# Surplus row products of the last pair beside the scores in the run-out of the L2 heads

## The chip, the cores and the metric

The kernel runs on one core of a Trainium2 chip (trn2). The metric is the device time in microseconds, taken as the median of several runs. The engines are named as the profile names them: PE is TensorE (matmul) and PEld its weight loads, DVE is VectorE, ACT is ScalarE, POOL is GpSimd, SP is SyncE, which issues the DMAs.

## The reference

Four conditioned blocks L0 to L3 are computed one after the other on `x` of shape (2, 1024, 256) in float32. The change lies in the attention heads of block L2 (16 heads of width 16, batch 2, sequence 1024):

```python
qkv = (h @ Wqkv.T + bqkv).reshape(B, N, num_heads, hd, 3)
q, k, v = ...                                     # each (B, 16, 1024, 16)
energy = jnp.einsum('bhqd,bhkd->bhqk', q, k)
att = jax.nn.softmax(energy, axis=-1) / D ** 0.5
out = jnp.einsum('bhqk,bhkd->bhqd', att, v)
out = jnp.moveaxis(out, 1, 2).reshape(B, N, D)
out = out @ Wp.T + bp
```

The rest of L2 (a conditioned norm ahead of it, and a residual with a second norm behind it) and the other three blocks (L0 a cumulative-sum attention, L1 attention and MLP, L3 attention with 16 heads of width 64 and a mixture of experts) are not touched.

## The kernel before, in words

The program is a chain of stages with a barrier of all engines between them. Stage `l2h` computes the L2 heads, class `NarrowPairs`; `layer2_out` follows it, and begins when the last result of the heads has been stored to DRAM.

There are B*H = 32 heads, taken in N = 16 pairs. The two heads of a pair lie on two halves of the partitions: head h = 0 on partitions 0 to 47, h = 1 on 64 to 111 (line 1425, `r = 64 * h`), so that TensorE can multiply for both at once, each on its own half of the array's rows. The contraction has 48 rows (`SPLIT`): the high and low parts of q and k in three blocks of 16.

Per pair m and tile of 128 rows (TB = 8 tiles) there are three kinds of work on TensorE:

- `row(m, t, h, c)`, lines 1424 to 1433: the products of 128 queries with 512 keys, into the double bank `rowb[h]`. DVE reduces each full `rowb[h]` (128x1024) to a negated maximum per query (line 1483, `maxes`). With c == 0 the product waits until DVE has read the bank's former content.
- `score(m, k, h, c)`, lines 1435 to 1442: the transposed products (128 keys by 512 queries, 50 rows: two more hold the maxima as a shift), into one of three banks `score`. ACT takes the exponential of each into `pT` (line 1516). A score product waits for the exponential of the bank's former content (`exps`).
- `mix(m, k)`, lines 1444 to 1455: exponentials times values, into bank `out`, over the whole 128 rows, 8 matmul instructions for one k.

The order on TensorE is written out in `pe_program`, lines 1457 to 1469: for each turn m from -2 to 16 and each k from 0 to 7 it issues, phase 0: row and score alternately for c = 0, 1, then `mix` of the k two steps back (`LAG`), then phase 1: row and score again for c = 0, 1. In a phase the row product is of head `phase` and the score product of head `1 - phase`, so the two lie on different halves of the rows. This is called a step below; it has four row products, four score products and one mix. Row products run 12 steps ahead of the scores (`ahead`, line 1368: the pair after next in the second half of a turn). So in turn 14 from k = 4 on and in turn 15, 12 steps in all, there are no row products left: `there(mr)` is false. These 12 steps, with the two mixes and the copy of the result (line 1501, `ocopy`) in turn 16, are called the run-out. When the last maximum of a pair is there, DVE turns the 16 columns of maxima (lines 1490 to 1495), and SP places them by eight small DMAs into the two extra rows of Q (line 1406, `place_shift`); the first score of the pair waits for them (line 1439).

GpSimd copies values (`staged`), early; ACT does the exponentials and one `ocopy` per pair; SP loads the pairs ahead, stores the results and places the shifts.

Of the kernel before, what the change touches and what calls it, by code (L numbers as in the profile page):

```python
# [21 lines left out]
P = 128  # L22
B, S, D = 2, 1024, 256
T = B * S // P
TB = S // P
KF = D // P
C = 512
# [1303 lines left out]
class NarrowPairs:  # L1331
# [91 lines left out]
    def pe_program(self, pe):  # L1423
        def row(m, t, h, c):
            u, r = m % self.SLOTS, 64 * h
            if c == 0:
                if t == 0:
                    pe.wait_ge(self.loaded[u], (m // self.SLOTS + 1) * 16 * self.LOADS)
                self.need(pe, self.maxes, (TB * m + t) * 2 + h - 1)
            mm = pe.matmul(self.rowb[h][:, c * C:(c + 1) * C], self.Q[r:r + self.SPLIT, u, t * P:(t + 1) * P],  # L1430
                           self.K[r:r + self.SPLIT, u, c * C:(c + 1) * C], start=True, stop=True)
            if c == 1:
                mm.then_inc(self.rowsums, 1)

        def score(m, k, h, c):
            u, r = m % self.SLOTS, 64 * h
            v = 4 * (TB * m + k) + 2 * (1 - h) + c
            if k == 0 and h == 1 and c == 0:
                pe.wait_ge(self.shifted, 8 * 16 * (m + 1))
            self.need(pe, self.exps, v - 2)  # L1440
            pe.matmul(self.score[v % 3][:, :], self.K[r:r + self.SPLIT + 2, u, k * P:(k + 1) * P],  # L1441
                      self.Q[r:r + self.SPLIT + 2, u, c * C:(c + 1) * C], start=True, stop=True).then_inc(self.scores, 1)

        def mix(m, k):
            g = TB * m + k
            pe.wait_ge(self.exps, 4 * (g + 1))
            if k == 0:
                pe.wait_ge(self.staged, m + 1)
                self.need(pe, self.ocopied, m)
            for h in range(2):  # L1450
                for c in range(2):
                    r = self.mw * (2 * h + c)
                    mm = pe.matmul(self.ob[r:r + self.mw, :], self.vs[:, m % self.SLOTS, h, k, :],  # L1453
                                   self.pT[:, g % 4, h, c * C:(c + 1) * C], start=k == 0, stop=k == TB - 1)
            mm.then_inc(self.mixed, 1)

        for m in self.TURNS:
            for k in range(TB):
                mr, tr = self.ahead(m, k)
                for phase in range(2):  # L1460
                    for c in range(2):
                        if self.there(mr):
                            row(mr, tr, phase, c)
                        if self.there(m):
                            score(m, k, 1 - phase, c)
                    if phase == 0:
                        mine, kk = (m, k - self.LAG) if k >= self.LAG else (m - 1, k - self.LAG + TB)
                        if self.there(mine):
                            mix(mine, kk)
# [1098 lines left out]
```

## Time and profile before

| | us |
|---|---|
| median of 3 runs | 2332.14 (2328.83 to 2342.71) |
| the profiled execution's own time | 2340.13 |
| its span in the trace | 2338.4 |
| PE busy | 1969.7 (84% of the span) |
| DVE busy | 1423.3 (61%) |
| ACT busy | 1117.9 (48%) |
| mean granted clock of TensorE | 0.896 |

A busy share is an average over stages with different limits; only the rows of the stage around the change tell what it is worth. PE is counted busy while a matmul is in flight, whatever part of the array it uses. PEclk is the granted clock of TensorE as a share of its full 2.4 GHz: 1.00 is 2.4 GHz, 0.50 is 1.2 GHz, and these are its two levels; a number between them in a window is a mixture. Times in rows are counted from the start of the span. The stage of the L2 heads goes from about 695 us to 1090 us.

### The profile page before, as it was taken

To read this page: it belongs to the slowest core of one execution; us is meant where nothing else is said; L and a number is where in the kernel's file an instruction comes from. 1 tells how busy PE (TensorE), PEld (TensorE's weight loads), DVE (VectorE), ACT (ScalarE), POOL (GpSimd) and SP (SyncE) were. 2 spreads that over 40 slices of the span, in tenths; PEclk is the share of its full clock that TensorE was granted. 3 is DMA by queue.
4 is the path that set the end of the run, shared out by engine and by line. 5 is a ranking of instruction groups with operands and counts; after the bars stand their busy time and mean duration, and the time that the engine had idled before them with its cause. 6 is when DMAs were issued, how large, how long until landed. Compare 5 with 4: busy or idle time off the path is not lost. (4 is left out here: it accounts for less than half of the span.)

```text
span 2338.4 us, 34514 instructions
## 1 busy us (share of the span) xinstructions
PE 1969.7 (84%) x12926; PEld 1155.3 (49%) x12926; DVE 1423.3 (61%) x2514; ACT 1117.9 (48%) x2013; POOL 737.9 (32%) x703
## 2 busy tenths in 40 slices
PE   6988589679649999995499949999999999794776
PEld 2444367568323333331345525555555555483676
DVE  5432543453448999960756638777777777317665
ACT  1111133231214888873256538777777777303243
POOL 2221340064003000001235535444444444103476
PEclk8999799889776999995699969999999999895688
DMA  5000000100143211102036783445444444242153
GB/s 158 0 1 0 16 7 1 38 1 1 54 135 99 47 36 49 49 7 77 7 116 216 221 223 86 113 113 113 113 113 111 110 109 109 91 149 103 31 160 81
DMA packets 197254, 190.96 MB, mean 82 GB/s; under 512 B 65440, under 2 KB 155936, under 8 KB 196832
## 3 DMA queue, kind: packets, MB, share of 16 engines
q1 hardware_dynamic: 194016, 184.56, 29.4%
q0 software_dynamic: 3072, 4.20, 0.9%
q8 instruction: 103, 1.69, 0.3%
q14 instruction: 63, 0.52, 0.1%
HBM read 121.07 MB, written 67.37 MB: 81 GB/s over the span
## 5 line engine op out<-in xcount | busy, mean ns | idle before, releaser
L1293 DVE TENSOR_REDUCE l3h_nmax<-l3h_score 128x1 f32<-128x1024 f32 x256 | 313.5, 1225 | 152.7 <-PE l3h_score L1236 152.7
L1327 POOL TENSOR_SCALAR l3h_prob<-l3h_prob,l3h_inv 128x1024 f32<-128x1024 f32 x256 | 288.3, 1126 | 340.6 <-DVE l3h_inv L1299 340.6
L1516 ACT ACTIVATE l2h_pT<-l2h_score 128x512 f32<-128x512 f32 x512 | 266.3, 602 | 118.6 <-PE l2h_score L1441 116.7
L1483 DVE TENSOR_REDUCE l2h_nm<-l2h_rowb 128x1 f32<-128x1024 f32 x256 | 301.0, 1217 | 31.8 <-PE l2h_rowb L1430 31.8
L1317 ACT ACTIVATE l3h_prob<-l3h_score,l3h_nmax 128x1024 f32<-128x1024 f32 x256 | 286.1, 1117 | 48.2 <-DVE l3h_nmax L1293 13.2
L1259 PE MATMUL l3h_out<-l3h_pT,l3h_vs 128*64 128x512 f32 x1024 | 274.4, 617 | 0.0
L1236 PE MATMUL l3h_score<-l3h_K,l3h_Q 64*128 64x512 f32 x1536 | 249.1, 430 | 26.2 <-DMA l3h_K<-l_k 24.3
L1236 PEld LDWEIGHTS l3h_score<-l3h_K,l3h_Q 64*128 64x128 f32 x1536 | 125.8, 186 | 238.0 <-issue 190.1
L1430 PE MATMUL l2h_rowb<-l2h_K,l2h_Q 48*128 48x512 f32 x512 | 183.0, 470 | 40.8 <-DMA l2h_K<-l_k 29.8
L1441 PE MATMUL l2h_score<-l2h_Q,l2h_K 50*128 50x512 f32 x512 | 206.0, 491 | 3.5 <-ACT l2h_pT L1516 3.5
L1285 ACT ACTIVATE l3h_pT<-l3h_ring 128x512 f32<-128x512 f32 x256 | 152.8, 597 | 100.9 <-PE l3h_ring L1247 100.4
L1247 PEld LDWEIGHTS l3h_ring<-ident,l3h_prob 64*128 64x128 f32 x4096 | 172.1, 139 | 37.0 <-issue 8.0
L1897 PE MATMUL l3qkv_bank<-w3qkvT,l3qkv_norm_out 128*128 128x512 f32 x384 | 174.4, 598 | 0.9 <-ACT l3qkv_norm_out L690 0.9
L1430 PEld LDWEIGHTS l2h_rowb<-l2h_K,l2h_Q 48*128 48x128 f32 x512 | 81.4, 199 | 189.1 <-DVE l2h_nm L1483 140.8
L1283 DVE COPY l3h_pT<-l3h_ring 128x512 f32<-128x512 f32 x256 | 172.1, 672 | 2.0 <-PE l3h_ring L1247 2.0
L1247 PE MATMUL l3h_ring<-ident,l3h_prob 64*128 64x64 f32 x4096 | 169.3, 222 | 2.2 <-DVE l3h_pT L1283 1.8
L1453 PE MATMUL l2h_out<-l2h_pT,l2h_vs 128*32 128x512 f32 x1024 | 148.2, 654 | 0.0
L1981 POOL TENSOR_TENSOR l3qkv_lo<-l3qkv_full,l3qkv_hi 128x512 fp32r<-128x512 f32 x64 | 102.3, 1625 | 133.6 <-ACT l3qkv_hi L1917 133.6
L1441 PEld LDWEIGHTS l2h_score<-l2h_Q,l2h_K 50*128 50x128 f32 x512 | 85.8, 195 | 63.3 <-ACT l2h_pT L1516 46.5
L1897 PEld LDWEIGHTS l3qkv_bank<-w3qkvT,l3qkv_norm_out 128*128 128x128 f32 x384 | 70.2, 192 | 72.8 <-issue 71.1
L1528 POOL COPY l2h_vs<-V 128x128 f32<-128x128 f32 x32 | 8.3, 294 | 255.3 <-PE l2h_out L1453 255.3
L1958 DVE TENSOR_SCALAR l3qkv_full<-l3qkv_bank,headln 128x512 f32<-128x512 f32 x64 | 50.5, 808 | 58.6 <-PE l3qkv_bank L1883 40.1
(355 smaller groups left out, 3364.3 us busy)
## 6 DMA issues: line engine op xcount, KB each, us to landing
l3h_Q<-l_q SPq DMA_DIRECT2D x128, 256.0 KB, 4.6
l3h_K<-l_k SPq DMA_DIRECT2D x128, 128.0 KB, 4.9
l_v<-l3qkv_v SPq DMA_DIRECT2D x16, 512.0 KB, 4.1
l_q<-l3qkv_hi SPq DMA_DIRECT2D x32, 256.0 KB, 2.8
l_q<-l3qkv_lo SPq DMA_DIRECT2D x32, 256.0 KB, 2.9
l_k<-l3qkv_hi SPq DMA_DIRECT2D x32, 256.0 KB, 3.7
l_k<-l3qkv_lo SPq DMA_DIRECT2D x32, 256.0 KB, 3.7
l3h_vs<-l_v SPq DMA_DIRECT2D x32, 256.0 KB, 3.5
```

Source lines behind the costliest of these rows:

```text
L1236: mm = pe.matmul(self.score[t % 2][:, c * C:(c + 1) * C], self.Q[r, u, x, t * P:(t + 1) * P], self.K[r, u, y, :], start=i == 0, stop=i == 2)
L1247: mm = pe.transpose(self.ring[half][:, kk * P // 2:(kk + 1) * P // 2], self.prob[r, g % 4, kk * P:(kk + 1) * P], self.ident[r, r])
L1259: mm = pe.matmul(self.ob[n % 2][c * self.hd:(c + 1) * self.hd, :], self.vs[:, n % 2, kk, :], self.pT[:, n % 2, kk, c * C:(c + 1) * C], sta ...
L1283: eng.tensor_copy(dst, src).then_inc(self.emptied_d, 1)
L1293: dve.tensor_reduce(self.nmax[:, t % 4:t % 4 + 1], self.score[t % 2][:, :], AX.X, ALU.max, negate=True).then_inc(self.maxes, 1)
L1317: act.activation(self.prob[:, q, :], self.score[g % 2][:, :], ACT.Exp, bias=self.nmax[:, q:q + 1], accum_out=self.total[:, q:q + 1]).then_ ...
L1327: pool.tensor_scalar(self.prob[:, q, :], self.prob[:, q, :], self.inv[:, q:q + 1], self.vscale, ALU.mult, ALU.mult).then_inc(self.scaled, 1)
L1430: mm = pe.matmul(self.rowb[h][:, c * C:(c + 1) * C], self.Q[r:r + self.SPLIT, u, t * P:(t + 1) * P], self.K[r:r + self.SPLIT, u, c * C:(c ...
L1441: pe.matmul(self.score[v % 3][:, :], self.K[r:r + self.SPLIT + 2, u, k * P:(k + 1) * P], self.Q[r:r + self.SPLIT + 2, u, c * C:(c + 1) * C ...
L1483: dve.tensor_reduce(self.nm[:, mr % 2, at:at + 1], self.rowb[h][:, :], AX.X, ALU.max, negate=True).then_inc(self.maxes, 1)
L1516: act.activation(self.pT[:, g % 4, h, c * C:(c + 1) * C], self.score[v % 3][:, :], ACT.Exp).then_inc(self.exps, 1)
L1897: mm = pe.matmul(bank[2 + j][:, :], nt.out[:, c, kf, t * P:(t + 1) * P], wT[:, (kf * 6 + j) * C:(kf * 6 + j + 1) * C], start=kf == 0, stop ...
```

## The change

A new function `again` in `pe_program` issues one row product of the last pair (m = 15, in slot 3), with no semaphore increment, into `rowb[h]`. It is called where a row product would stand, for the steps in which none is left but scores are: the pair index `mr` is 16 or 17 and m is 14 or 15. These are 12 steps with four products each, 48 in all. Each is preceded by a wait until DVE has made all 256 maxima, which is after the last read of `rowb`. The operands are those of earlier row products of pair 15, and the results are not read.

```diff
@@ -1432,6 +1432,12 @@
             if c == 1:
                 mm.then_inc(self.rowsums, 1)
 
+        def again(t, h, c):
+            u, r = (self.N - 1) % self.SLOTS, 64 * h
+            pe.wait_ge(self.maxes, 2 * TB * self.N)
+            pe.matmul(self.rowb[h][:, c * C:(c + 1) * C], self.Q[r:r + self.SPLIT, u, t * P:(t + 1) * P],
+                      self.K[r:r + self.SPLIT, u, c * C:(c + 1) * C], start=True, stop=True)
+
         def score(m, k, h, c):
@@ -1461,6 +1467,8 @@
                     for c in range(2):
                         if self.there(mr):
                             row(mr, tr, phase, c)
+                        elif mr >= self.N and self.there(m):
+                            again(tr, phase, c)
                         if self.there(m):
                             score(m, k, 1 - phase, c)
```

## Rows read from the trace of the kernel before

**Rows 1.** Page, the span in 40 slices of 58.5 us

```profile
PE   6988589679649999995499949999999999794776
PEclk8999799889776999995699969999999999895688
```

**Rows 2.** Windows: us; busy PE, PEld, DVE, ACT, POOL; PEclk, DMA share, GB/s

```profile
744.00:1036.00 292.00, 285.89 (x1768) 100.53 (x1765) 265.18 (x260) 235.47 (x454) 6.38 (x24) 1.00 0.17 41
...
1036.00:1042.00 6.00, 4.89 (x29) 1.43 (x25) 1.94 (x5) 4.74 (x10) 0.00 (x0) 1.00 0.01 1
1042.00:1086.00 44.00, 41.55 (x135) 10.36 (x135) 0.00 (x0) 21.83 (x43) 0.00 (x0) 0.50 0.02 4
```

**Rows 3.** Waits between 1042 and 1086 us, the longest

```profile
ACT l2h_pT L1516 <- PE l2h_score L1441: 17.8, 9, 2.0
```

**Rows 4.** Timeline around the last row products: start us, us, engine, line

```profile
1033.57 2.07 ACT L1516 ACTIVATE l2h_pT<-l2h_score 128x512 f32<-128x512 f32 x4 [0.54 <-PE l2h_score L1441]
...
1034.64 1.07 PE L1453 MATMUL l2h_out<-l2h_pT,l2h_vs 128*32 128x512 f32 x8
...
1035.64 0.49 PE L1430 MATMUL l2h_rowb<-l2h_K,l2h_Q 48*128 48x512 f32 x1
...
1035.64 0.49 PE L1441 MATMUL l2h_score<-l2h_Q,l2h_K 50*128 50x512 f32 x1
...
1036.17 2.07 ACT L1516 ACTIVATE l2h_pT<-l2h_score 128x512 f32<-128x512 f32 x4 [0.54 <-PE l2h_score L1441]
1036.40 1.23 DVE L1483 TENSOR_REDUCE l2h_nm<-l2h_rowb 128x1 f32<-128x1024 f32 x1 [0.24 <-PE l2h_rowb L1430]
...
1036.83 0.50 PE L1441 MATMUL l2h_score<-l2h_Q,l2h_K 50*128 50x512 f32 x1 [0.24 <-ACT l2h_pT L1516]
...
1037.25 1.06 PE L1453 MATMUL l2h_out<-l2h_pT,l2h_vs 128*32 128x512 f32 x8
...
1038.25 0.73 PE L1441 MATMUL l2h_score<-l2h_Q,l2h_K 50*128 50x512 f32 x3
1038.31 5.21 SPq L1406 DMA_DIRECT2D l2h_Q<-l2h_shift  x8
...
1039.87 1.06 PE L1453 MATMUL l2h_out<-l2h_pT,l2h_vs 128*32 128x512 f32 x8
```

**Rows 5.** Timeline of the run-out at the low clock, and its end

```profile
1046.74 1.94 PE L1453 MATMUL l2h_out<-l2h_pT,l2h_vs 128*32 128x512 f32 x8
...
1048.61 1.22 PE L1441 MATMUL l2h_score<-l2h_Q,l2h_K 50*128 50x512 f32 x3
...
1079.27 1.94 PE L1453 MATMUL l2h_out<-l2h_pT,l2h_vs 128*32 128x512 f32 x8
...
1081.97 1.08 ACT L1516 ACTIVATE l2h_pT<-l2h_score 128x512 f32<-128x512 f32 x2 [1.99 <-PE l2h_score L1441]
...
1085.99 0.60 ACT L1501 ACTIVATE l2h_osb<-l2h_out 128x512 f32<-128x512 f32 x1 [2.94 <-PE l2h_out L1453]
```

**Rows 6.** Copies of the result at line 1501, one per pair, steady

```profile
1009.25 0.60 ACT L1501 ACTIVATE l2h_osb<-l2h_out 128x512 f32<-128x512 f32 x1
1030.48 0.60 ACT L1501 ACTIVATE l2h_osb<-l2h_out 128x512 f32<-128x512 f32 x1
```

**Rows 7.** Timeline of PE in the run-in of the stage

```profile
731.48 0.79 PE L1430 MATMUL l2h_rowb<-l2h_K,l2h_Q 48*128 48x512 f32 x1 [0.17 <-DVE l2h_nm L1483]
731.49 0.79 PE L1441 MATMUL l2h_score<-l2h_Q,l2h_K 50*128 50x512 f32 x1
...
732.64 1.93 PE L1453 MATMUL l2h_out<-l2h_pT,l2h_vs 128*32 128x512 f32 x8
...
736.71 1.86 PE L1453 MATMUL l2h_out<-l2h_pT,l2h_vs 128*32 128x512 f32 x8
738.50 0.50 PE L1430 MATMUL l2h_rowb<-l2h_K,l2h_Q 48*128 48x512 f32 x1
```

## The prediction

> **What bounds the kernel now.** I read the page's forty slices first [rows 1]. TensorE is the busiest engine, and its granted clock is full in most slices; the eighteenth and nineteenth slice, which reach from 994 to 1111 us, show PEclk fall to 9 and 5. The change lies at the end of the L2 heads, so I cut that stretch into windows [rows 2]. From 744 to 1036 us, while row products, scores and mixes all run, the clock is 1.00 (2.4 GHz) without a break. From 1036 to 1042 us it is still 1.00, with TensorE busy 4.89 of 6 us: there the last row products have just gone. From 1042 to 1086 us it is 0.50 (1.2 GHz), DVE does nothing, and ACT is busy 21.8 of 44 us. The list of waits names what ends last there: ACT waits 17.8 us in nine pieces of up to 2.0 us for a score product [rows 3]. In the run-out TensorE at the low clock sets the pace, and ACT, which has the same four exponentials per step as before, idles for half of it.
>
> The timeline gives the price of a step. Up to the last row products the mixes start at 1034.64 and 1037.25 us, a step of 2.61 us; the first step without row products is 1037.25 to 1039.87, 2.62 us, still at the full clock [rows 4]. So the row products cost nothing while they are there: a row and a score product begin together at 1035.64 and both take 0.49 us, on the two halves of the rows [rows 4]. What limits a step at the full clock is the loop of ACT and TensorE: four exponentials take 2.07 us and are followed by 0.54 us of waiting for the next score, 2.61 together [rows 4]. At the low clock the mixes at 1046.74 and 1079.27 us lie eight steps apart, 4.07 us each [rows 5]: a mix takes 1.94 us instead of 1.06 and three scores 1.22 instead of 0.73 [rows 4, 5].
>
> **The change part by part.** Nothing is removed and nothing moved; 48 products and 48 waits are added to TensorE's queue, none to another queue.
>
> First, the clock. After the change TensorE does in each of the 12 steps just what it did in the steady part: four products of 48 rows on one half, four scores on the other, a mix. In the steady part that held 1.00 for 292 us [rows 2], and in the run-in, row and score pairs with a mix between them at 732.64 us stood ahead of the rise, which the trace shows at 738.50, where a row product takes 0.50 instead of 0.79 us [rows 7]. Without the row products the clock fell about six us after the last of them. I take it that 1.00 holds to the last step. The mix of turn 15, k = 7 comes 11 steps after the one at 1037.25. At 2.61 us these are 28.7 us, and 0.1 more for the one copy of a result among them, so it would start at 1066.05 instead of 1079.27: 13.2 us less. The steady pitch of whole pairs, 1030.48 less 1009.25 = 21.23 us for eight steps, is 2.65 per step [rows 6] and would give 12.8; it holds row waits on DVE that the run-out has not, so I take 13.2 and keep 12.8 as an end.
>
> Second, the end. From that last stepped mix to the copy of the last result it is now 6.72 us (1079.27 to 1085.99) [rows 5]. At the full clock: 1.00 us from mix to the next scores (1037.25 to 1038.25), 0.53 from the score to its exponential (1035.64 to 1036.17) [rows 4], 1.08 for the two exponentials [rows 5], about 0.25 until the last mix begins (the 0.24 that stands beside the score at 1036.83) and 1.06 for it [rows 4], near 4.0 in all. That takes off 2.7 us. No added product stands in this piece; it is within 4 us of the last one, and the clock lasted longer than that after the last row products before. If it fell at once, 2.7 would become zero.
>
> Third, the added wait. The first surplus product stands right behind the last row and score pair, and waits for the 256th maximum. DVE begins that reduction at 1036.40 and needs 1.23 us, to 1037.63 [rows 4]. Queued behind the waiting product are both scores of head 1, the mix, and all that follows; ACT waits for these scores. Now the second of them starts at 1036.83 and the mix 0.42 later, at 1037.25 [rows 4]. With the wait: first pair at 1037.7, second about 0.33 later, mix another 0.42 later, 1038.45, so 1.2 us late, once. ACT has two exponentials left of its four at that time, which end at 1037.2, so nothing hides the rest. The ends are 0.9 (ACT picks up part of it) and 1.5. The other 47 waits find the count already there. The eight DMAs that place the last shift are issued from 1038.31 to 1043.5 [rows 4]; the first score that needs them now comes near 1037.25 + 1.2 + 4 x 2.61 - 1.2 = 1047.7 us, so they stay ahead of it, as they are for every earlier pair at this pitch.
>
> Fourth, the 48 products themselves. Each lies beside a score, on the half of the rows that the score does not use; the rows just read price them at nothing at the full clock, and at the low clock too: the pair at 731.48 and 731.49 us runs side by side at 0.79 each, and the step from 732.64 to 736.71 with row products is 4.07 us, the same as without [rows 5, 7]. If that cover failed and each took its turn, three scores in 0.73 us make 0.24 each [rows 4], 48 of them 11.7 us. Zero it is, with 11.7 as the far end. They write banks which nobody reads, so DVE gets no work from them. The Trainium skill (TensorEngine Tiling (Array Packing), Instruction Overhead) speaks against the change here: it gives each matmul about 60 cycles of overhead on trn2, which by its figure would be an estimated 1.2 us for 48 at 2.4 GHz, and the sum below would be 13.5 instead of 14.7; the equal steps with and without row products (2.61 and 2.62 us) disagree with paying it here.
>
> The sum: 13.2 + 2.7 - 1.2 = 14.7 us saved. Against the profiled execution that is 2340.13 - 14.7 = 2325.4 us. It is 8 us above the median of the runs shown, and the run-out has no part in that difference that I could see, so I take the saving off the median: 2332.14 - 14.7 = **2317.4 us**, 0.6% less. Layer2_out starts when the last result is stored, so the whole saving passes on to it.
>
> **The rivals.**
>
> A. The clock dips once and comes back. For it: the new wait leaves TensorE idle for about 1.1 us just where row products ended, and the clock may be granted by what it did in that stretch. Against: the clock never fell in the 292 us with this mixture, and after the last row products it took some six us to fall, much longer than this wait. In the run-in the clock came back within two steps of the first mix [rows 7]. Two to four steps at 4.07 instead of 2.61 us cost 2.9 to 5.8 us: 2320 to 2323 us.
>
> B, on the slower side. The clock falls anyway, because what lowers it is not the missing row products; then it is 0.50 in the run-out as now, steps are 4.07 us with or without them, and the wait is all that remains: 2332.1 + 1.2 = 2333.3 us. It decides if the clock falls within about a step of where it fell before. For it: the cause of the fall is inferred from one place. Against: 292 us with the same mixture and no fall. Here the rule that the Trainium skill states bears (TensorE: Matmul & The Clock Gate, Part 1: The HAM clock gate), that the clock follows how busy TensorE has recently been and falls after idleness. By it, products inside time that already counts as busy would change nothing, which is this rival; but the trace has the clock at 0.50 with TensorE busy 41.55 of 44 us [rows 2], so busy time as the profile counts it is not what decides, and the rule in that reading has little for it here.
>
> C, slower for good. The clock falls, and the surplus products take turns with the scores. At the low clock three scores take 1.22 us, 0.41 each [rows 5]; 48 are 19.5 us, with the wait 20.7: 2352.8 us. The side-by-side pair at the low clock [rows 7] is against it. At the full clock the same failure leaves 14.7 - 11.7 = 3.0 us of gain, 2329 us.
>
> D. More than forecast: the later stage also starts at a better clock. After the run-out comes a stretch with no matmul, so I see no carrier for it. A gain over 1% (23 us) would need 8 us from elsewhere; only scatter between runs could give it.
>
> **How the numbers follow.** Chances: the forecast 0.78, A 0.09, B 0.06, C 0.03 with both of its clocks, D 0.04. A measurement of this kernel can tell about 1%, 23 us, from no change; the forecast, A and B all lie within it. The runs of before lie between 3.3 us under and 10.6 us over their median, so the forecast's median can lie some 5 us off, and the ends of the terms (12.8, 0 to 2.7, 0.9 to 1.5) add from -0.3 to +3.4. Downwards this gives 2317 - 5 - 0.3 with a little of D, 2308; upwards it takes in A with that scatter, 2323 + 6 = 2329. Left out are B, the worse half of C and a part of D, about 0.12. Faster by over 1% gets 0.05, slower 0.03, the rest, 0.92, is within 1%.
>
> **What would show it.** Right: PEclk 1.00 in windows from 1042 to about 1068 us; mixes every 2.61 us in the run-out; row-shaped products in number 560 at two lines of the kernel instead of 512; one idle stretch of PE and ACT of about a microsecond after the last reduction; the last copy at line 1501 near 1071 us instead of 1086, and everything after it earlier by the same 14.7 us. Wrong: a granted clock of 0.50 in the run-out (A if for two to four steps, B if to the end), steps over 2.7 us with a clock of 1.00 (C), score products starting 0.2 us or more behind their partners. A shift of the later stages against each other by more than two or three us would mean that their clocks, which change in the middle of them, have fallen differently, and would blur the total but not the run-out.

## The result and the profile after

The changed kernel takes 2328.46 us in the median of 22 executions (2325.13 to 2332.33), the kernel before, timed beside it, 2332.97 us (22 executions, 2327.04 to 2342.71). The ratio is 0.9979 with a 95% interval of 0.997 to 0.9989: 4.5 us faster, where 14.7 were forecast. The profiled executions differ by more: 2340.13 us before, 2327.20 us after, 12.9 us.

The page's slices of the changed kernel, against [rows 1]: PEclk in the nineteenth slice is 8 instead of 5.

```profile
PE   6988589769649999996499949999999999794776
...
PEclk8999799889876999998699969999999999895688
```

The windows of the run-out, with the columns of [rows 2]:

```profile
1038.00:1040.00 2.00, 0.86 (x8) 0.50 (x12) 1.65 (x4) 1.04 (x3) 0.00 (x0) 0.96 0.00 0
1040.00:1043.00 3.00, 3.00 (x14) 1.14 (x8) 0.00 (x0) 1.26 (x4) 0.00 (x0) 0.50 0.01 2
1044.00:1073.00 29.00, 28.91 (x188) 10.74 (x180) 0.00 (x0) 22.80 (x45) 0.00 (x0) 1.00 0.03 6
```

The clock is 1.00 from 1044 us to the end of the heads, where before it was 0.50 for 44 us. But there is a dip: at 1040 to 1043 us it is 0.50. The timeline shows what stands ahead of it (start, duration, engine, line; L1438 is the surplus product, L1447 a score, L1459 a mix, L1491 DVE's reduction, L1509 the copy):

```profile
1037.43 0.39 PE L1447 MATMUL l2h_score<-l2h_Q,l2h_K 50*128 50x512 f32 x1
1037.63 1.08 ACT L1524 ACTIVATE l2h_pT<-l2h_score 128x512 f32<-128x512 f32 x2 [0.55 <-PE l2h_score L1447]
1037.86 1.23 DVE L1491 TENSOR_REDUCE l2h_nm<-l2h_rowb 128x1 f32<-128x1024 f32 x1 [0.26 <-PE l2h_rowb L1430]
...
1039.14 0.49 PE L1438 MATMUL l2h_rowb<-l2h_K,l2h_Q 48*128 48x512 f32 x1 [1.31 <-DVE l2h_nm L1491]
...
1039.14 0.49 PE L1447 MATMUL l2h_score<-l2h_Q,l2h_K 50*128 50x512 f32 x1
...
1039.80 1.93 PE L1459 MATMUL l2h_out<-l2h_pT,l2h_vs 128*32 128x512 f32 x8
...
1043.62 1.07 PE L1459 MATMUL l2h_out<-l2h_pT,l2h_vs 128*32 128x512 f32 x8
...
1069.81 1.06 PE L1459 MATMUL l2h_out<-l2h_pT,l2h_vs 128*32 128x512 f32 x8
...
1073.62 0.60 ACT L1509 ACTIVATE l2h_osb<-l2h_out 128x512 f32<-128x512 f32 x1 [1.19 <-PE l2h_out L1459]
```

The first surplus product starts at 1039.14, as DVE's last reduction ends at 1037.86 + 1.23 = 1039.09; TensorE stood still for 1.31 us. The mix behind it runs at the low clock (1.93 us), the next one at the full clock (1.07 us), one step of 3.82 us. Then ten steps take 26.19 us, 2.62 each, and surplus product and score begin together. From the start of the last reduction to the last copy it is now 35.8 us (1037.86 to 1073.62), against 49.6 in [rows 4, 5] (1036.40 to 1085.99). The difference of 13.8 us passes on: from the last copy to the last result of the experts it is 242.4 us in the profile before and 241.8 in the one after.

So between the two profiles the run-out is shorter by what was forecast within a microsecond (13.8 for 14.7 us), their totals within two (12.9 us), and the medians are not. The question is not where the gain went in the changed kernel, but whether the kernel before pays in each execution what its profile showed.

### The profile page after: what moved, and what is told of

It reads as the page before. It is cut to its first block and busy times, and to the rows that moved or that the text cites. A ratio compares the mean times of both kernels' runs of the same rounds, so it can differ in the third digit from the quotient of the medians.

```text
span 2325.5 us, 34610 instructions
## 1 busy us (share of the span) xinstructions
PE 1960.3 (84%) x12974; PEld 1160.1 (50%) x12974; DVE 1422.6 (61%) x2514; ACT 1117.1 (48%) x2013; POOL 732.8 (32%) x703
## 5 line engine op out<-in xcount | busy, mean ns | idle before, releaser
L1491 DVE TENSOR_REDUCE l2h_nm<-l2h_rowb 128x1 f32<-128x1024 f32 x256 | 301.1, 1217 | 31.8 <-PE l2h_rowb L1430 31.8
L1447 PE MATMUL l2h_score<-l2h_Q,l2h_K 50*128 50x512 f32 x512 | 201.4, 469 | 0.1
L1459 PE MATMUL l2h_out<-l2h_pT,l2h_vs 128*32 128x512 f32 x1024 | 138.7, 614 | 0.0
L1447 PEld LDWEIGHTS l2h_score<-l2h_Q,l2h_K 50*128 50x128 f32 x512 | 85.2, 188 | 38.8 <-ACT l2h_pT L1524 37.9
```

Source lines behind the costliest of these rows:

```text
L1491: dve.tensor_reduce(self.nm[:, mr % 2, at:at + 1], self.rowb[h][:, :], AX.X, ALU.max, negate=True).then_inc(self.maxes, 1)
```

## The experiments

A step without row products is called thin below, and the stretch ahead of the run-out, with row products in each step, dense. All lengths called the run-out go from the start of the last reduction of `l2h_rowb` to the start of the last copy to `l2h_osb`.

### The kernel before, run again

The kernel of before, unchanged (no diff).

> The kernel before, unchanged, for how its own executions spread. Theory 1 (the fall of the clock in the run-out comes in only a part of the executions of the kernel before, and the profiled one was such): times fall into a lower group near 2328 us with a mean clock near 0.90 and an upper one near 2339 us with 0.896; the profile shows the run-out either at 0.50 for 44 us or mostly at 1.00, when from the last row product to the last copy it takes about 37 us instead of 50. Theory 2 (the clock always falls there, and most executions of the changed kernel lose time in later stages): one group, the run-out 50 us long at 0.50 in this profile too, and every total near 2333 us.

Measured: median 2334.58 us over 12 executions, 2327.76 to 2345.07; the kernel before beside it 2331.19 us over 28; ratio 1.001 (0.9992 to 1.0027). The mean clock of an execution goes with its time, 0.901 and 0.903 in the two shortest, 0.893 in the longest. The profiled execution took 2327.76 us. Two windows of its thin steps, the last copy and the last reduction (windows, then the list by instruction with duration min/median/max and first and last start):

```profile
1040.00:1044.00 4.00, 3.09 (x20) 0.95 (x16) 0.21 (x1) 2.93 (x7) 0.00 (x0) 1.00 0.01 2
...
1064.00:1068.00 4.00, 3.10 (x20) 0.90 (x22) 0.00 (x0) 3.21 (x7) 0.00 (x0) 1.00 0.00 0
```

```profile
L1501 ACT ACTIVATE l2h_osb<-l2h_out x16: 597/597/600, 756.4 to 1071.7; 128x512 f32<-128x512 f32 x16
```

```profile
L1483 DVE TENSOR_REDUCE l2h_nm<-l2h_rowb x256: 1181/1217/1227, 698.5 to 1038.3; 128x1 f32<-128x1024 f32 x128
```

The same kernel, the same thin steps, and the clock stays at 1.00 to the end: the run-out is 1071.7 - 1038.3 = 33.4 us, 16.2 less than in the first profile. The fall of the clock does not belong to each execution of the kernel before; it comes in a part of them. Theory 1 stands, though not in its form of two clean groups: the times between 2328 and 2340 us are filled.

### The changed kernel, run again

> The changed kernel, unchanged. Theory 1: ratio about 0.998 as before, its run-out again 36.5 us long with at most one or two steps at 0.50, and behind the heads the same stage lengths as in the first two profiles within 1 us. Theory 2: the same ratio, but this profile shows a later stage (the one behind the heads, or the experts) some 5 to 10 us longer than in the first profile of it, at a lower clock.

Measured: median 2329.99 us over 12 executions (2327.39 to 2332.46), ratio 0.9988 (0.9975 to 1.0001). The run-out is 35.8 us again, with the same dip:

```profile
1041.00:1046.00 5.00, 4.85 (x24) 2.05 (x28) 0.66 (x4) 2.65 (x6) 0.00 (x0) 0.66 0.01 2
1046.00:1075.00 29.00, 28.92 (x188) 10.74 (x180) 0.00 (x0) 22.74 (x45) 0.00 (x0) 1.00 0.03 6
```

From the last copy to the last result of the experts it is 243.1 us, 1.3 more than in the first profile of it, and no stage in it is more than 1.4 us longer. No later stage gives back 5 to 10 us: theory 2 falls. Over all 34 executions of this kernel none is above 2332.5 us.

### The wait alone

```diff
         def again(t, h, c):
             u, r = (self.N - 1) % self.SLOTS, 64 * h
             pe.wait_ge(self.maxes, 2 * TB * self.N)
-            pe.matmul(self.rowb[h][:, c * C:(c + 1) * C], self.Q[r:r + self.SPLIT, u, t * P:(t + 1) * P],
-                      self.K[r:r + self.SPLIT, u, c * C:(c + 1) * C], start=True, stop=True)
```

> The wait for the 256th maximum at its place, without any surplus product: it prices the wait. Both theories: at least the 1.2 us of the wait, ratio 1.0005, if the clock does what it did before. Theory 1 adds that the pause ahead of the thin stretch makes the fall surer or earlier: up to 9 us slower than before, ratio up to 1.004. Theory 2: no more than 1.2 us.

Measured: median 2349.98 us, all six executions between 2347.52 and 2352.55; ratio 1.007 (1.0053 to 1.0086). The run-out is 53.7 us. Windows of its profile:

```profile
1036.00:1040.00 4.00, 2.70 (x18) 0.77 (x17) 3.15 (x6) 2.51 (x6) 0.00 (x0) 0.99 0.00 0
1040.00:1044.00 4.00, 3.65 (x16) 0.98 (x12) 0.00 (x0) 2.58 (x6) 0.00 (x0) 0.50 0.02 3
```

The six times lie close together and none is near the kernel before's: the pause of 1.3 us with thin steps behind it seems to bring the fall in each execution, in the profile in the first step, and nothing brought the clock back: 20.3 us over a run-out without a fall, 1.1 of them the wait itself. It is more than theory 1 had given it, since I had reckoned from the first profile as the usual case. Its steps at the low clock are 4.13 us (mixes at 1043.35 and 1084.62 us, ten steps apart) instead of 4.07 [rows 5]; over ten steps that is 0.6 us more, with a wait ahead of each score that the kernel before does not have. It also shows what the surplus products do in the changed kernel: its pause is the same, and there the low clock lasts one step instead of twelve.

### The pause taken away

The products of head 0 wait for the last reader of their own bank alone.

```diff
         def again(t, h, c):
             u, r = (self.N - 1) % self.SLOTS, 64 * h
-            pe.wait_ge(self.maxes, 2 * TB * self.N)
+            pe.wait_ge(self.maxes, 2 * TB * self.N - 1 + h)
```

> The surplus products of head 0 wait for the 255th maximum (the last reader of their own bank), those of head 1 for the 256th, so that the pause of 1.3 us before the first of them goes. Both theories: 1.0 to 1.4 us less than the changed kernel for the wait. If the one step at the low clock in the changed kernel's profile came from that pause, another 1.5 to 2 us: about 3 us less than the changed kernel, ratio to before about 0.9968; the run-out from the last row product to the last copy 33.5 us instead of 36.5, with 1.00 throughout.

Measured: median 2328.03 us over 11 executions, ratio to before 0.9975 (0.9962 to 0.9987). The run-out is 33.5 us, without a dip:

```profile
1042.00:1075.00 33.00, 32.87 (x206) 12.04 (x205) 1.30 (x4) 25.66 (x50) 0.00 (x0) 1.00 0.03 6
```

The profiled execution took 2334.0 us all the same, 6.8 more than the first profile of the changed kernel, since other stretches were longer in it: 3.0 us up to the first score (at 730.8 instead of 727.8 us), 0.6 from there to the last reduction (310.7 instead of 310.1), and 5.3 from the last copy to the last result of the experts (247.1 instead of 241.8), of these 2.2 in the products of `layer2_out` (27.0 instead of 24.8). Over the profiles of all kernels here but the last one below, the total less the run-out goes from 2290.5 to 2300.5 us, so an execution can differ by up to 10 us for reasons outside the run-out. One of them is the clock again, at the other end of the stage: in the run-in it rises near 735 us in one profile (`before_look2`, 9 us after the first score) and near 747 in another (`quarter_surplus` below, 18 us after it). Once more, beside other kernels:

> bank_wait once more, beside the others on one chip: 33.4 us from the last maximum to the last copy, no fall, about 5 us under the kernel before, ratio 0.998 or less.

Median 2329.31 us over 8, ratio 0.9966 (0.9952 to 0.998), run-out 33.5 us, no dip. Over the 19 executions of both the mean is 2328.0 us, against 2329.1 over 34 of the changed kernel. The 2.3 us between the run-outs (35.8 and 33.5) are seen in the profiles; in the totals 1.1 us is left, and with standard deviations of 3.0 and 2.2 us it is not clear of the spread.

### More profiles of the kernel before

> A third profile of the kernel before. So far one had the low clock from the third step of the run-out to its end (49.6 us from the last maximum to the last copy), one never (33.4 us). Theory A (the fall can come at any step of the thin stretch, and then stays): a length anywhere between 33.4 and 50, by the step where it falls. Theory B (it is decided once, where the row products end): 33.4 or about 50, nothing between.

> A fourth profile of the kernel before. The first three had 49.6, 33.4 and 44.9 us from the last maximum to the last copy, with the clock falling in the third step, never, and in the fifth. Theory A (a fall possible at any thin step, then lasting): again any length from 33.4 to 50, equal to 33.4 + 1.45 for each step behind the fall + 2.7 at the end.

Measured: 2336.72 and 2337.93 us, one execution each; the run-out is 44.9 us in both. The timeline of the first of them where the clock falls:

```profile
1044.36 1.06 PE L1453 MATMUL l2h_out<-l2h_pT,l2h_vs 128*32 128x512 f32 x8
1045.35 0.73 PE L1441 MATMUL l2h_score<-l2h_Q,l2h_K 50*128 50x512 f32 x3
1046.54 0.50 PE L1441 MATMUL l2h_score<-l2h_Q,l2h_K 50*128 50x512 f32 x1 [0.45 <-ACT l2h_pT L1516]
1046.96 1.07 PE L1453 MATMUL l2h_out<-l2h_pT,l2h_vs 128*32 128x512 f32 x8
1047.96 0.73 PE L1441 MATMUL l2h_score<-l2h_Q,l2h_K 50*128 50x512 f32 x3
1049.14 0.63 PE L1441 MATMUL l2h_score<-l2h_Q,l2h_K 50*128 50x512 f32 x1 [0.45 <-ACT l2h_pT L1516]
1049.70 1.93 PE L1453 MATMUL l2h_out<-l2h_pT,l2h_vs 128*32 128x512 f32 x8
```

The sixth mix of the run-out is the first slow one here, where in the first profile it was the third. Steps do not differ before it: the fall comes out of the same pattern that had run at the full clock for five steps. The length follows: from this mix to the last stepped one are six steps, 33.4 + 6 x 1.45 + 2.7 = 44.8 us, and nine in the first profile, 49.2 against 49.6 measured. (The expectation counts the step in which the fall lies, the fifth.) Theory A stands, and theory B falls with the lengths between 33.4 and 50: a fall can come early, later or not at all, and in the three profiles that had it the clock did not return before the last mix.

### Where the surplus work is needed, and how much

In four kernels, all with the wait of `bank_wait`, the condition under which `again` is called is changed. Each line with a plus below is that of one kernel:

```diff
-                        elif mr >= self.N and self.there(m):
+                        elif mr >= self.N and self.there(m) and c == 0:                    # half_surplus
+                        elif mr >= self.N and self.there(m) and c == 0 and phase == 0:     # quarter_surplus
+                        elif mr >= self.N and m == self.N - 2:                             # first_four
+                        elif mr >= self.N and m == self.N - 1 and k >= 4:                  # last_four
                             again(tr, phase, c)
```

> Surplus products in the first four steps of the run-out alone (the rest of turn 14), with the wait of bank_wait; eight thin steps follow. Theory A: the clock still falls in a part of the executions, later: excess up to 8 x 1.45 + 2.7 = 14.3 us, mean about 2331 to 2332. Theory B in its form that the end of DVE's work or the edge at turn 14 matters: as bank_wait, 2328.

> Surplus products in the last four steps of the run-out alone, behind eight thin ones. Where the clock falls in the thin steps, do the surplus products bring it back? If so: falls cost at most 8 steps of 1.45 less what comes before the fall, and about one to two of the last four steps, no 2.7 us at the end; no execution above 2341, mean about 2331. If not: as before, 2333, with executions up to 2345.

> Surplus products for c == 0 alone (24 instead of 48), with the wait of bank_wait. If how much work is beside the scores decides how surely the clock holds, half of it helps in part: mean between before (2333) and bank_wait (2328), some executions over 2335. If any work there is enough: as bank_wait, 2328, and the profile at 1.00 throughout with 33.5 us.

> Surplus products for head 0, c == 0 alone: 12 instead of 48, one in each step. If any more work in the step is enough: as half_surplus, 2328. If the clock's hold grades with it: some executions fall, mean 2329 to 2332, a few above 2335.

| | products | executions | mean us | highest us | above 2335 us | ratio to before, interval |
|---|---|---|---|---|---|---|
| kernel before, all comparisons | 0 | 104 | 2333.8 | 2345.1 | 40 | |
| first_four | 16 | 10 | 2333.2 | 2338.8 | 4 | 0.9997 (0.9982 to 1.0013) |
| last_four | 16 | 10 | 2331.7 | 2341.9 | 2 | 0.9993 (0.9976 to 1.001) |
| quarter_surplus | 12 | 12 | 2329.6 | 2333.1 | 0 | 0.9978 (0.9968 to 0.9989) |
| half_surplus | 24 | 8 | 2327.9 | 2333.7 | 0 | 0.9966 (0.995 to 0.9983) |
| bank_wait, both runs | 48 | 19 | 2328.0 | 2334.0 | 0 | 0.9975 and 0.9966 |
| the changed kernel | 48, paused | 34 | 2329.1 | 2332.5 | 0 | 0.9979 and 0.9988 |

The executions come from several comparisons on more than one chip, and a ratio is to the kernel before on the same chip. The border of 2335 us is a rough one: the longest execution of these kernels whose profile shows no fall took 2334.0 us, and the shortest total outside the run-out, 2290.5, with a run-out of 44.9 us makes 2335.4. So what lies above it most likely had a fall by the sixth mix or so, and a later fall can hide below it.

Sixteen products in the first four steps alone bought nothing that can be told from zero: with eight thin steps behind them four of ten executions were above 2335 us still. Twelve, one in each step, kept all twelve executions below it. So it is rather the place that decides than the count, as it would be if the clock can fall in any thin step; with ten and twelve executions this is likely and not certain. The mean of `quarter_surplus` lies in the 2329 to 2332 us written down for a hold that grades with the work, but with none above 2335 us, and 1.6 us over `bank_wait` is not clear of the spread (standard error about 1 us); whether a quarter holds the clock quite as surely as the whole is open. The mean of `first_four` is a microsecond over what was expected, with ten executions too few to make anything of it. `last_four` was meant to show whether the products bring the clock back; neither its profile nor that of `first_four` had a fall (33.4 us each), and its one execution at 2341.9 us is just above the bound of 2341 that I had given. That recovery is seen only in the changed kernel's two profiles. The windows of nearly the whole run-out at half and then at a quarter:

```profile
1038.00:1071.00 33.00, 30.27 (x184) 10.00 (x182) 1.65 (x4) 26.00 (x51) 0.00 (x0) 1.00 0.02 5
```

```profile
1041.00:1074.00 33.00, 30.38 (x172) 9.95 (x170) 1.74 (x4) 26.09 (x51) 0.00 (x0) 1.00 0.02 5
```

### The pause put into the dense part

```diff
             if c == 0:
                 if t == 0:
                     pe.wait_ge(self.loaded[u], (m // self.SLOTS + 1) * 16 * self.LOADS)
-                self.need(pe, self.maxes, (TB * m + t) * 2 + h - 1)
+                self.need(pe, self.maxes, (TB * m + t) * 2 + h - 1 + (t == 0 and h == 0))
```

> bank_wait, with the first row product of each pair waiting for the last maximum of the pair before it, as the first surplus product of the changed kernel does: some 14 pauses of about 1.3 us in the dense part, each with row products behind it. If such a pause alone costs its 1.2 us: 14 x 1.2 = 17 us over bank_wait, 2345 us, and PEclk 1.00 throughout. If each brings about one step at the low clock as in the two profiles of the changed kernel (2.3 us in all): 32 us over bank_wait, 2360 us, with some 14 short falls of the clock in the windows.

Measured: 2350.64 us in the median of five executions, but in two groups: 2341.8 and 2342.0 with a mean clock of 0.903 and 0.904, and 2350.6, 2351.1 and 2357.6 with 0.896, 0.896 and 0.892. The profiled one is of the lower group. One of its pauses, and the windows of the whole dense part:

```profile
786.72 1.23 DVE L1491 TENSOR_REDUCE l2h_nm<-l2h_rowb 128x1 f32<-128x1024 f32 x1 [0.25 <-PE l2h_rowb L1430]
...
788.10 0.47 PE L1430 MATMUL l2h_rowb<-l2h_K,l2h_Q 48*128 48x512 f32 x1 [1.41 <-DVE l2h_nm L1491]
```

```profile
745.00:1050.00 305.00, 286.72 (x1770) 102.43 (x1767) 267.68 (x259) 235.59 (x455) 6.41 (x24) 1.00 0.16 39
```

From the first score to the last reduction it is 325.3 us instead of the 310.7 of both profiles of bank_wait, 14.6 us for 14 pauses: 1.04 each. The first of them, ahead of 742.17 us, lies in the run-in, where the clock is still 0.50. The other 13 lie in the window shown, and the clock stayed at 1.00 through all of these. So a pause of this length does not bring a dip every time, neither of the two answers that I had written down is right alone, and the group 9 to 16 us higher, at a lower mean clock, is what dips in some of the pauses would look like; no profile of that group was taken. Why both profiles of the changed kernel had the dip and this one none in thirteen pauses at the full clock stays open.

## Why the prediction was wrong

**What bounds the kernel.** That the run-out at 0.50 is paced by TensorE and costs 4.07 us a step was read rightly, of one execution. That the kernel before is always bounded so was the mistake: of its four profiles the low clock came at the third mix in one, at the sixth in two, and not at all in one.

**The clock, 13.2 us, and the end, 2.7 us.** For the execution profiled the terms hold: steps of 2.62 us, and 3.8 us from the last stepped mix to the last copy where 4.0 were forecast. The size of the pair failed as a difference of medians. The kernel with nothing in its way (bank_wait) has a mean of 2328.0 us and a run-out of 33.5; the kernel before 2333.8. A run-out without a fall is 33.4 us there too, so an average execution loses 5.8 us to the falls, not 15.9 or 16.2. The 5.8 is a difference of totals, not a count of falls; but 40 of 104 executions above 2335 us, where the kernels with surplus products in each step have none, say the same.

**The step that failed** stands in the sum: the profiled execution was 8 us above the median, "and the run-out has no part in that difference that I could see, so I take the saving off the median". It had all the part: against the profiled execution without a fall the run-out was 16.2 us longer (49.6 and 33.4), and everything outside it 3.9 us shorter (2290.5 and 2294.4). The 8 us and the 14 us between the lowest and highest of only three runs were the sign that something in this kernel comes in some executions and not in others, and the one thing in the trace that could be either was the clock level in a stretch that had been at 1.00 for its first two steps. The saving could be taken off the profiled execution (forecast 2325.4, measured 2327.2), not off the median. That these two totals come so close is in part luck, with up to 10 us of difference outside the run-out; the run-out itself (34.9 and 35.8 us) is the fair comparison. Luck too is that the measured 2328.46 us lies inside the range of 2308 to 2329: its upper end came from rival A and the scatter of the runs, and not from a fall that is absent in a part of the executions before.

**The added wait, 1.2 us.** Measured 1.1: the mix behind it starts 3.70 us after the one before it (1036.10 to 1039.80) instead of 2.61. But it brought **rival A** with it: the low clock for one step, 3.82 instead of 2.61 us, 1.2 us more, in both profiles. I had priced that rival at two to four steps and put it behind the forecast; in the trace it stood beside it. The run-out overshot the forecast of 34.9 us by 0.9: 1.2 for this dip, less 0.1 of the wait and 0.2 of the end.

**The 48 products at nothing.** Right at the full clock: 2.62 us a step with them and 2.61 to 2.62 without; no profile has a whole step with them at the low clock. They are not free on TensorE, they are covered. Before, three scores in a row take 0.73 us (from 1038.25 on [rows 4]); after, they take 0.95 (1044.62 to 1045.57). But the fourth starts 1.19 us after the first before, where it waits for ACT, and 1.18 after:

```profile
1039.44 0.50 PE L1441 MATMUL l2h_score<-l2h_Q,l2h_K 50*128 50x512 f32 x1 [0.46 <-ACT l2h_pT L1516]
```

```profile
1044.62 0.49 PE L1447 MATMUL l2h_score<-l2h_Q,l2h_K 50*128 50x512 f32 x1
...
1044.95 0.62 PE L1447 MATMUL l2h_score<-l2h_Q,l2h_K 50*128 50x512 f32 x2
...
1045.80 0.50 PE L1447 MATMUL l2h_score<-l2h_Q,l2h_K 50*128 50x512 f32 x1
```

That the clock holds with them was right too, in every profile behind the dip. The Trainium skill's overhead for each matmul (TensorEngine Tiling (Array Packing), Instruction Overhead), an estimated 1.2 us for the 48, is not seen in the run-out: 48 products (33.5 us) and none at the full clock (33.4 us) make the same length within 0.1 us. Since ACT's pace covers what the products add, this does not show that they have no overhead.

**Rival B** (something else lowers the clock) falls: row-shaped work that nobody reads kept it up in all six profiles behind the dip or without one, and of the 73 executions of the four kernels that had it in each step (and no pauses elsewhere) none was above 2335 us, where 40 of 104 without it were. The Trainium skill's rule that idleness lowers the clock (TensorE: Matmul & The Clock Gate, Part 1: The HAM clock gate), read as idleness alone, does not tell these executions apart: the clock fell in the kernel before after a window with TensorE busy 3.13 of 4 us (1038 to 1042, no gap over 0.46), while it held in another execution through the windows above with 3.09 and 3.10 of 4 us. **C** falls with the side-by-side starts (1039.14 us for both products), **D** with a stretch behind the heads of 241.8 us after and 242.4 before. What makes the clock fall in one execution and not in the next is not shown.

## What to carry to other kernels

A stretch in which TensorE has less to do than in the steady part can run at either clock from one execution to the next, so one profile gives the size of the loss but not how often it comes; look at the spread of the timed runs and at how the profiled one lies in it before a saving is taken off the median. What is bought by filling such a stretch is then as much steadiness as time: the standard deviation went from 4.2 to 2.2 us (3.0 for `bank_wait`), the mean down by 4.7. And surplus work should wait for no more than the last reader of its own bank: here the longer wait cost 2.3 of the 16 us that it can save in an execution with an early fall.

## What was not expected of the hardware

- The granted clock fell from 1.00 to 0.50 out of a pattern of equal steps (1.06 us of mix, four scores, gaps of 0.45 to 0.54 us) after two steps, after five steps, or in none of twelve, in executions of the same program.
- Once down, it stayed down under that same pattern to the end of the run-out, 6 to 9 steps of 4.07 us, in three profiles, and eleven in that of `wait_only`; with the surplus products beside, it returned within one step, in both profiles that had a fall with them.
- With one product more per step, 12 in 33 us, none of twelve executions was above 2335 us, and the one profiled held 1.00.
- A pause of 1.3 to 1.4 us stood right ahead of a fall in all three profiles where it lay at the beginning of the run-out, and ahead of none in thirteen places of the dense part, in the one profile taken there.
- The rise at the start of the stage wanders too: from 0.50 to 1.00 near 735 us in one profile and near 747 in another, 9 and 18 us after the first score.
